# Projections and scores of an attention's first part, placed between the steps of the MLP in front of it

## The chip, the core and the metric

The kernel runs on one core of a Trainium2 chip. The metric is the device time of one execution in microseconds. Engines: TensorE (PE, its weight loads PEld), VectorE (DVE), ScalarE (ACT), GpSimd (POOL), SyncE (SP, which here issues all DMAs).

## The reference, cut to what matters

Four small transformer blocks run one after the other on x of 4 batches x 256 rows x 256 columns. Only the order and the shapes bear on this case.

```python
x = L0(ctx, x)      # 16-head attention over 512 keys, rms norm, MLP (m0)
x = L1(x, ctx)      # two attentions with 16 heads of 128 (b11, b12), layer norm, MLP (m1)
# L2, all heads 16 wide:
h = layernorm(x, ln1)                       # norm l21
q, k, v = split(h @ w_qkv + b_qkv)          # self attention: parts 0 to 3 of stage a2
s = q @ k.T / sqrt(16); s = s * mask - 10000 * (1 - mask)
x = x + softmax(s) @ v @ w_ao + b_ao
h = layernorm(x, ln2)                       # norm l22
x = x + attention(h @ w_q, enc @ w_kv, cross_mask) @ w_co   # parts 4 to 7 of a2
x = x + gelu(layernorm(x, ln3) @ w1) @ w2   # norm l23, MLP m2
# L3: no norm ahead of it
q, k, v = x @ Wq, enc @ Wk, enc @ Wv        # 32 query heads of 8, 8 key heads: stage a3
x = layernorm(softmax(q @ k.T / sqrt(8) + mask) @ v @ Wo + x)
```

## The kernel before, in words

Everything stays in SBUF; x lies as rows in `x_rows`, and what feeds a projection lies transposed in `hT`. The stages follow each other as a0, m0, b11, b12, m1, a2, m2, a3. Each engine has its own program, and semaphores tie them; the order on each engine is written out by hand.

**A small-head attention** (`attention(c)`, one function on each engine; `SMALL[1]` is a2 with 8 parts, `SMALL[2]` is a3 with 4) works on parts, one batch each, and a part on units: 16 in a2, 32 in a3, 128 in all in both. TensorE's `slot(s)` issues at slot s: scores of four units if s is a multiple of 4 (`scores`, L532, into banks 0 to 3, once the earlier four are out of them), the transposes of a unit some slots older (L545, banks 4 and 5), the product with v of four units (`times_v`, L567, bank 6), and, at fixed places of a part, the projections q, k and v of the next part (`project`, L502, L511, L517) and the output projection (L585). In a2 VectorE multiplies the scores with the mask (`times_mask`, L1103, four units at once) and takes the maxima (`maxima`, L1121); in a3 the mask is added, by L1121 alone. ScalarE does the exponentials (`exps`, L888) and copies the transposed units (`turned`, L896); VectorE shares the copies in a3 (L1129). VectorE also evacuates q (`queries`, L1067) and v (`values`, L1085), ScalarE k (`keys`, L875). All projections but those of part 0 go through bank 7, and so do the transposed rows of a norm: who comes next waits until the one before is evacuated (`before(m)`, `free`). `bank_of(m)` gives the banks of part 0: q 7, k 6, v 4.

**The host.** The MLP in front leaves the rows of its last batch normed (`norm_rows`, L1041; for a3 there is no norm) but not transposed. The attention does it (`c.host`, `normed(slot)`): slot 0 issues the four transposes (L464, bank 7), and ScalarE copies them to `hT` (`take_rows`, L856) after its first exponentials. Part 1's q projection, at slot 3 in a2 and slot 2 in a3, needs bank 7 and so this copy.

**An MLP** (`mlp`) runs over 4 batches, and over 10 steps f of each: steps 0 to 7 issue the first layer's tile f (L655, bank f mod 4; ScalarE's gelu, L921), steps 2 to 9 the second layer's tile f - 2 (L666, banks 4 and 5). At step 5 of a batch the normed rows of the batch before are transposed through bank 7. m2 also issues, in its batch 0, the last slots of a2. VectorE adds the result to `x_rows` (L1213) and takes its statistics (L1007, L1012, L1022). Only when m1 or m2 is through, and its last gelu and addition too, does TensorE begin the attention with q, k, v of part 0.

**POOL** does, in a fixed order, the power of each norm (L1354), the addition of a bias row to `x_rows` (L1349) and the conversion of a mask into its additive form (`additive`, L1343, L1345). SP loads the masks once the maxima that used the buffer are done.

## Time and profile before

| | us |
|---|---|
| median of 3 runs | 1602.65 |
| lowest, highest | 1600.52, 1605.79 |
| the profiled execution | 1607.07 |
| its span, first to last instruction | 1605.0 |

| engine | busy us | share of the span |
|---|---|---|
| TensorE matmul | 1493.2 | 93% |
| VectorE | 949.4 | 59% |
| ScalarE | 908.1 | 57% |
| POOL | 85.3 | 5% |

The shares are means over stages with different limits; the rows below go stage by stage. m1 ends at about 1073 us of the span, a2 runs to about 1326, m2 to about 1391, a3 to the end. A busy TensorE is one whose pipeline holds a matmul; the 0.17 us by which a group of matmuls seems to overlap the next is its latency. The short `READ_ACCUMULATOR` instructions between the maxima and exponentials are part of them.

### The profile page before, as it was taken

What the parts mean: (1) busy time and instruction counts of PE and PEld (TensorE: products, weight loads), DVE (VectorE), ACT (ScalarE), POOL (GpSimd) and SP (SyncE); (2) the same over time, 40 slices, a digit from 0 to 9 for tenths busy, and PEclk for the clock granted to TensorE, in tenths of its full rate; (3) what the DMA queues carried; (4) which work ended last, traced back from release to release, by engine and by line L of the source; (5) the groups of instructions that cost most, each with busy time, mean ns of one, the idle gap of its engine ahead of it and who ended that gap; (6) DMA issues with size and microseconds to landing.
All of it is one profiled execution on the core that took longest, in us unless ns stands there. A gap on an engine that the chain in (4) does not pass through costs nothing.

```text
span 1605.0 us, 28634 instructions
## 1 busy us (share of the span) xinstructions
PE 1493.2 (93%) x9824; PEld 1146.4 (71%) x9824; DVE 949.4 (59%) x3398; ACT 908.1 (57%) x2803; POOL 85.3 (5%) x89
## 2 busy tenths in 40 slices
PE   7999999999999999999999999997888879888886
PEld 5666687788787777778787878775656557755554
DVE  4777624545454455544455455238999991278885
ACT  5788824444444344444344444327888884388896
POOL 2000010000000001000000000110010010100000
PEclk9999999999999999999999999998999999999998
DMA  7000103010100101001010000010001000000000
GB/s 283 2 2 2 62 1 118 1 47 15 47 15 1 61 1 60 1 1 60 1 61 1 1 0 1 1 53 1 2 1 41 8 8 7 0 2 8 21 2 14
DMA packets 10878, 40.64 MB, mean 25 GB/s; under 512 B 2416, under 2 KB 2672, under 8 KB 8688
## 3 DMA queue, kind: packets, MB, share of 16 engines
q1 hardware_dynamic: 10736, 38.82, 6.8%
q8 instruction: 80, 1.31, 0.3%
q14 instruction: 62, 0.51, 0.1%
HBM read 37.77 MB, written 1.05 MB: 24 GB/s over the span
## 4 chain that ended last, share of the span: by engine, by line
PE 68%; DVE 11%; ACT 6%; issue 5%; DVEq 0%; POOLq 0%; POOL 0%; ACTq 0%
PE bank L726 7%; PE bank L707 7%; PE bank L740 7%; PE bank L699 7%; PE bank L686 7%; PE bank L689 7%; PE bank L666 5%; PE bank L655 5%; PE bank L715 4%; PE bank L545 3%; DVE probs L1121 3%; ACT probs L888 3%; DVE probs L1103 3%; PE bank L532 3%; DVE q_res L1067 2%
## 5 line engine op out<-in xcount | busy, mean ns | idle before, releaser
L888 ACT ACTIVATE probs<-probs,negmax 128x256 f32<-128x256 f32 (+1 forms) x640 | 346.9, 549 | 78.3 <-DVE negmax L1121 77.9
L959 ACT ACTIVATE pT<-bank 128x512 f32<-128x512 f32 x128 | 76.5, 597 | 387.8 <-PE bank L715 387.8
L545 PEld LDWEIGHTS bank<-ident,probs 128*128 128x128 f32 x1536 | 175.5, 145 | 110.6 <-issue 55.1
L545 PE MATMUL bank<-ident,probs 128*128 128x128 f32 x1536 | 232.4, 287 | 23.1 <-DVE pT L1129 12.5
L1236 DVE TENSOR_REDUCE stats<-bank 128x1 f32<-128x257 f32 x256 | 108.4, 425 | 212.4 <-PE bank L707 211.4
L1121 DVE CUSTOM_DVE_ANT_0 probs<-bank,mask_a 128x256 f32<-128x256 f32 (+1 forms) x384 | 176.2, 508 | 37.6 <-PE bank L532 33.4
L896 ACT ACTIVATE pT<-bank 128x512 f32<-128x512 f32 x304 | 178.1, 587 | 33.1 <-PE bank L545 32.9
L726 PE MATMUL bank<-pT,probs 128*128 128x256 f32 x512 | 132.6, 381 | 2.7 <-ACT pT L959 2.7
L707 PE MATMUL bank<-kT,pT 128*128 128x257 f32 x512 | 132.7, 382 | 0.6 <-ACT pT L942 0.6
L532 PE MATMUL bank<-kT,q_res 32*128 32x256 f32 (+1 forms) x1280 | 114.8, 465 | 17.0 <-DVE negmax L1121 13.8
L888 ACT ACTIVATION_READ_ACCUMULATOR probs<-probs,negmax 128x1 f32 x640 | 126.1, 197 | 0.0
L950 ACT ACTIVATE probs<-bank,stats 128x257 f32<-128x257 f32 x256 | 118.7, 474 | 3.5 <-DVE stats L1239 3.5
L726 PEld LDWEIGHTS bank<-pT,probs 128*128 128x128 f32 x512 | 95.8, 190 | 19.5 <-ACT pT L959 3.7
L707 PEld LDWEIGHTS bank<-kT,pT 128*128 128x128 f32 x512 | 96.3, 190 | 17.9 <-issue 3.2
L921 ACT ACTIVATE pT<-bank,cols 128x256 f32<-128x256 f32 x96 | 45.1, 474 | 107.7 <-PE bank L655 107.6
L1121 DVE CUSTOM_DVE_ANT_0 probs<-probs,mask_a 128x256 f32<-128x256 f32 x256 | 102.4, 451 | 0.0
L655 PE MATMUL bank<-hT,w_m 128*128 128x256 f32 x384 | 96.4, 382 | 1.3 <-DVE negmax L1121 1.3
L666 PE MATMUL bank<-w_m,pT 128*128 128x256 f32 x384 | 95.2, 379 | 0.3 <-ACT pT L921 0.3
L532 PEld LDWEIGHTS bank<-kT,q_res 32*128 32x128 f32 x1280 | 58.8, 192 | 45.4 <-issue 22.0
L1354 POOL TENSOR_TENSOR rstd<-ms,half 128x2 f32<-128x2 f32 x32 | 23.3, 729 | 1221.7 <-DVE ms L1022 1107.7
L1103 DVE TENSOR_TENSOR probs<-bank,mask_m 128x512 f32<-128x512 f32 x128 | 79.3, 681 | 9.8 <-PE bank L532 9.8
L1250 DVE TENSOR_SCALAR probs<-probs,stats 128x257 f32<-128x257 f32 x256 | 79.0, 351 | 4.5
(107 smaller groups left out, 2445.1 us busy)
## 6 DMA issues: line engine op xcount, KB each, us to landing
w_m<-in_w SPq DMA_DIRECT2D x6, 1024.0 KB, 7.1
g_qkv<-in_g SPq DMA_DIRECT2D x4, 1536.0 KB, 7.3
q_res<-in_g SPq DMA_DIRECT2D x4, 1536.0 KB, 6.3
w_qkv<-in_w SPq DMA_DIRECT2D x3, 768.0 KB, 4.3
g_bv<-in_gbv SPq DMA_DIRECT2D x8, 256.0 KB, 6.7
g_o<-in_go SPq DMA_DIRECT2D x4, 512.0 KB, 3.4
q_res<-in_go SPq DMA_DIRECT2D x4, 512.0 KB, 3.4
rows<-in_rows SPq DMA_DIRECT2D x1, 1664.0 KB, 14.0
```

Source lines behind the costliest of these rows:

```text
L532: last = mm(out, q_res[at, p % 2, i * c.res + r, q * P:(q + 1) * P], kT[at, p % 2, i % c.ktiles, 0:c.kv * P], start=True, stop=True)
L545: last = nc.tensor.transpose(out[:, n * P:(n + 1) * P], probs[:, u % PROBS, q * T + t * P:q * T + (t + 1) * P], ident[:, :])
L655: last = mm(bank[f % 4][:, 0:T], w_m1[:, k, f * P:(f + 1) * P], hT[:, b, k, :], start=(k == 0), stop=(k == KT - 1))
L666: last = mm(bank[4 + q][:, 0:D], h1T[:, f - 2, q * P:(q + 1) * P], w_m2[:, f - 2, :], start=(f == 2), stop=(f == FT + 1))
L686: mm(out[:, 0:T], g_qkv[g % 2][:, 1, k, h * P:(h + 1) * P], ctxT[:, b, k, :], start=(k == 0), stop=(k == KT - 1))
L707: mm(bank[q][:, 0:K1], qT1[:, n % 2, q * P:(q + 1) * P], kT1[:, n % 2, :], start=True, stop=True).then_inc(sem("b_scores"), 1)
L726: last = mm(bank[PV_BANK][:, 0:T], v1[:, u % 2, t, h * P:(h + 1) * P], pT1[:, n % 2, t, :], start=(t == 0), stop=(t == QT - 1))
L888: last = nc.scalar.activation(s, s, ACT.Exp, bias=negmax[:, u % PROBS, k:k + 1], scale=-1.0, accum_out=sums[:, tile % 2, q, j * c.res + r: ...
L896: nc.scalar.activation(pT[:, u % TURNED, :], bank[4 + u % 2][:, :], ACT.Copy).then_inc(sem("a_tout"), 1)
L950: last = nc.scalar.activation(probs1[:, n % 2, q, :], bank[q][:, 0:K1], ACT.Exp, bias=stats1[:, n % 2, 1, q:q + 1], scale=scale, accum_out ...
L1103: v.tensor_tensor(probs[:, u % PROBS, :], bank[u % QUAD][:, :], mask_m[:, mask_side(p), :], ALU.mult).then_inc(sem("a_masked"), 1)
L1121: last = v.tensor_tensor_reduce(out[:, at], src[:, at], mask_a[:, mask_side(p), at], -c.scale, HIGHEST, ALU.add, ALU.min, negmax[:, u % PR ...
```

## The change

For a2 and a3, TensorE issues the projections of part 0 between the steps of the last batch (b = 3) of the MLP in front: q at steps 1 and 2, k at 3 and 4, v at 7 and 8, and slot 0 (scores of units 0 to 3) at step 9, ahead of the last second-layer matmuls. Part 0 now has q in bank 6, k in 7, v in 6. ScalarE empties k behind the gelu of step 4, and TensorE waits for that before it transposes rows in bank 7 at step 5. VectorE empties q and v ahead of the last batch's addition. The host's rows are transposed at slot 10 instead of slot 0; in a2 VectorE norms them at its slot 3, behind the products of units 4 to 7, and makes the products of units 0 to 3 one by one between the maxima. POOL's order is written by slots: the host's bias comes with slot 12, the masks of a3 for batches 0 and 1 are converted at slots 117 and 133 of a2 instead of late in m2. The first exponentials of a tile wait for `a_inv` instead of `a_recip`. The waits of TensorE for the MLP's last gelu and addition move to step 9 and to the first transposes; the waits for the weights and for `s_rows` move ahead of the MLP.

```diff
     def normed(self, slot):
-        got = [-1] if slot == 0 and self.host else []
+        got = [-1] if slot == 10 and self.host else []
...
     def bank_of(self, m):
-        return [7, 6, 4, 5, 7][m] if m < len(self.loads()) else 7
+        return ([6, 7, 6] if self.host else [7, 6, 4, 5, 7])[m] if m < len(self.loads()) else 7
...
# TensorE, slot(s), at s == c.turn_lag
+                        else:
+                            pe.wait_ge(sem("m_out"), end("m1" if c.name == "2" else "m2", "m_out", B))
...
# TensorE, mlp, at each step f
                                 rows_turned(pe, own, b - 2)
+                            if b == B - 1 and project:
+                                k = S["a2" if n == 1 else "a3"]
+                                pe.wait_ge(sem("a_kout"), k.at("a_kout", 0, 1))
                             turn_rows(own, b - 1, bank[7])
+                        if b == B - 1 and project:
+                            if f == 1:
+                                if n == 1:
+                                    pe.wait_ge(sem("b_oout"), end("b12", "b_oout"))
+                                else:
+                                    pe.wait_ge(sem("a_oout"), end("a2", "a_oout"))
+                                project("q", 0, 0)
+                            elif f == 2:
+                                project("q", 0, 1)
+                            elif f == 3:
+                                rows_turned(pe, own, b - 2)
+                                project("k0", 0, 0)
+                            elif f == 4:
+                                project("k0", 0, 1)
+                            elif f == 7:
+                                project("v0", 0, 0)
+                            elif f == 8:
+                                project("v0", 0, 1)
+                            elif f == 9:
+                                pe.wait_ge(sem("m_gelu"), st.at("m_gelu", b, FT))
+                                following(0)
...
# ScalarE, exps
                     if tile >= 2 and u % (c.units // 2) == 0:
-                        act.wait_ge(sem("a_recip"), st.at("a_recip", 0, tile - 1))
+                        act.wait_ge(sem("a_inv"), st.at("a_inv", 0, tile - 1))
...
# ScalarE, mlp, behind the gelu of step f
+                        if b == B - 1 and f == NORM_AT - 1 and keys:
+                            keys("k0", 0)
...
# VectorE, attention
-                queries(0)
-                if c.host:
-                    norm_rows(c.host, B - 1, x_rows)
...
                 if c.kinds == "mult":
-                    for u in range(QUAD):
-                        times_mask(u)
+                    times_mask(0)
                 for slot in range(c.last_slot() + 1):
                     if slot < c.count:
                         maxima(slot)
-                        if c.kinds == "mult" and slot % QUAD == 3 and slot + 1 < c.count:
+                        if c.kinds == "mult" and slot < 3:
+                            times_mask(slot + 1)
+                        elif c.kinds == "mult" and slot % QUAD == 3 and slot + 1 < c.count:
                             for u in range(slot + 1, slot + 1 + QUAD):
                                 times_mask(u)
+                    if slot == 3 and c.host:
+                        norm_rows(c.host, B - 1, x_rows)
...
# VectorE, mlp
                         norm_rows(own, b - 1, x_rows)
+                    if b == B - 1 and queries:
+                        queries(0)
+                        values("v0", 0)
                     added(dve, f"m{n}", b)
...
# POOL
+            def after2(slot):
+                c = SMALL[1]
+                if slot == 12:
+                    pool.wait_ge(sem("l_z"), S["l21"].at("l_z", 0, B))
+                    bias("o2s", B - 1)
+                    additive(c, "2c", 0)
...
+                for b, x in enumerate([7 * c.units, 8 * c.units]):
+                    if slot == x + 5:
+                        additive(SMALL[2], "3", b)
...
+            def after3(slot):
+                c = SMALL[2]
+                if slot == 12:
+                    pool.wait_ge(sem("l_t"), S["l3t"].at("l_t", 0, B))
+                    bias("o3", B - 1)
...
```

## Rows read from the trace of the kernel before

**Rows 1.** Windows of three stretches: length, busy of PE, PEld, DVE, ACT, POOL, clock.

```profile
1040.00:1073.50 33.50, 33.50 (x160) 29.15 (x158) 5.38 (x18) 11.27 (x24) 3.93 (x4) 1.00 0.01 1
...
1090.50:1122.00 31.50, 25.98 (x239) 18.47 (x236) 30.50 (x111) 26.81 (x89) 0.00 (x0) 0.99 0.01 1
...
1409.50:1440.00 30.50, 26.23 (x266) 18.17 (x270) 24.86 (x119) 29.06 (x104) 0.00 (x0) 0.94 0.01 2
```

**Rows 2.** Timeline in MLP m1: start, us, engine, line, operation, [idle before, releaser].

```profile
1062.54 1.03 PE L655 MATMUL bank<-hT,w_m 128*128 128x256 f32 x4
...
1063.40 1.03 PE L666 MATMUL bank<-w_m,pT 128*128 128x256 f32 x4
1063.60 0.47 ACT L921 ACTIVATE pT<-bank,cols 128x256 f32<-128x256 f32 x1 [1.25 <-PE bank L655]
```

**Rows 3.** Timeline of the seam from m1 to a2.

```profile
1070.74 2.75 PE L666 MATMUL bank<-w_m,pT 128*128 128x256 f32 x12
...
1075.69 0.17 DVE L1022 TENSOR_SCALAR ms<-mv 128x2 f32<-128x2 f32 x1
...
1078.35 0.84 ACT L875 ACTIVATE kT<-bank,cols 128x256 f32<-128x256 f32 x2 [6.93 <-PE bank L511]
1078.44 0.73 DVE L1041 TENSOR_SCALAR y_rows<-x_rows,mv,rstd 128x256 f32<-128x256 f32 x2
...
1079.97 1.15 PE L532 MATMUL bank<-kT,q_res 32*128 32x256 f32 x16
...
1081.05 0.65 PE L464 MATMUL bank<-ident,y_rows 128*128 128x128 f32 x4
1081.21 2.48 DVE L1103 TENSOR_TENSOR probs<-bank,mask_m 128x512 f32<-128x512 f32 x4 [0.25 <-PE bank L532]
...
1085.41 1.00 ACT L856 ACTIVATE hT<-bank,cols 128x256 f32<-128x256 f32 x2
...
1086.46 2.07 PE L502 MATMUL bank<-hT,w_qkv 128*128 128x256 f32 x4 [4.76 <-ACT hT L856]
...
1088.47 2.09 PE L532 MATMUL bank<-kT,q_res 32*128 32x256 f32 x16
...
1090.57 2.48 DVE L1103 TENSOR_TENSOR probs<-bank,mask_m 128x512 f32<-128x512 f32 x4 [4.12 <-PE bank L532]
...
1094.78 0.42 DVE L1121 CUSTOM_DVE_ANT_0 probs<-probs,mask_a 128x256 f32<-128x256 f32 x1
```

**Rows 4.** Timeline of the seam from m2 to a3.

```profile
1388.81 2.75 PE L666 MATMUL bank<-w_m,pT 128*128 128x256 f32 x12
...
1395.34 1.00 PE L517 MATMUL bank<-w_qkv,ctxT 128*128 128x64 f32 x8
...
1398.61 1.15 PE L532 MATMUL bank<-kT,q_res 32*128 32x256 f32 x16 [2.27 <-DVE q_res L1067]
...
1399.85 0.42 DVE L1121 CUSTOM_DVE_ANT_0 probs<-bank,mask_a 128x256 f32<-128x256 f32 x1 [0.74 <-PE bank L532]
...
1402.64 0.63 ACT L856 ACTIVATE hT<-bank 128x256 f32<-128x256 f32 x2
...
1405.80 2.09 PE L532 MATMUL bank<-kT,q_res 32*128 32x256 f32 x16
1405.91 3.71 DVE L1067 TENSOR_SCALAR q_res<-bank,cols,marks 128x256 f32<-128x256 f32 x8 [3.21 <-PE bank L502]
...
1409.54 0.41 DVE L1121 CUSTOM_DVE_ANT_0 probs<-bank,mask_a 128x256 f32<-128x256 f32 x1
```

**Rows 5.** Window after the longest TensorE wait of the seam; last but two: granted clock.

```profile
1086.40:1088.40 2.00, 1.94 (x4) 1.17 (x4) 0.05 (x2) 1.98 (x9) 0.00 (x0) 0.50 0.00 0
```

**Rows 6.** Timeline of ScalarE in a2: the end of its packed stretch.

```profile
1121.62 0.51 ACT L888 ACTIVATE probs<-probs,negmax 128x256 f32<-128x256 f32 x1 [1.46 <-DVE negmax L1121]
```

**Rows 7.** Timelines of POOL and of VectorE, one moment in a2.

```profile
1208.01 0.85 POOL L1343 TENSOR_SCALAR mask_a<-mask_m 128x512 f32<-128x512 f32 x1 [6.04 <-DMA mask_m<-in_mask_2c]
...
1208.30 0.83 DVE L1121 CUSTOM_DVE_ANT_0 probs<-probs,mask_a 128x256 f32<-128x256 f32 x1
```

More of the change, by code:

```diff
@@ L620, in slot, with mlp @@
                             project(what, p, n)
-                for what in c.loads():
-                    project(what, 0, 0)
-                    project(what, 0, 1)
-                return slot
-            def mlp(n, before, own, after=None, c=None):
+                if c.name == "0":
+                    for what in c.loads():
+                        project(what, 0, 0)
+                        project(what, 0, 1)
+                return slot, project
+            def mlp(n, before, own, after=None, c=None, following=None, project=None):
                 st = S[f"m{n}"]
@@ L822, in _ @@
             c = SMALL[0]
-            slot = attention(c)
+            slot, _ = attention(c)
             for s in range(c.count + 2):
@@ L877, in keys, with attention @@
                     last.then_inc(sem("a_kout"), 1)
+                return keys
+            def attention(c):
+                st, keys = S["a" + c.name], keys_of(c)
                 def exps(u):
@@ L896, in turned @@
                     nc.scalar.activation(pT[:, u % TURNED, :], bank[4 + u % 2][:, :], ACT.Copy).then_inc(sem("a_tout"), 1)
-                for what in c.loads():
-                    if what[0] == "k":
-                        keys(what, 0)
+                if c.name == "0":
+                    for what in c.loads():
+                        if what[0] == "k":
+                            keys(what, 0)
                 for slot in range(c.count + c.copy_lag):
@@ L913, in attention, with mlp @@
                             keys(what, p)
-            def mlp(n, gelu, before, own):
+            def mlp(n, gelu, before, own, keys=None):
                 st = S[f"m{n}"]
@@ L1086, in values, with attention @@
                     last.then_inc(sem("a_pout"), 1)
+                return queries, values
+            def attention(c):
+                st = S["a" + c.name]
+                queries, values = projections_of(c)
+                dst = y_rows if c.name == "0" else x_rows
                 def mask_side(p):
@@ L1200, in attention, with mlp @@
                                 values(what, p)
-            def mlp(n, before, own):
+            def mlp(n, before, own, queries=None, values=None):
                 st = S[f"m{n}"]
@@ L1384, in _ @@
                 power_and_bias("l1m", b, "m1")
+            def after2(slot):
+                c = SMALL[1]
+                if slot == 12:
+                    pool.wait_ge(sem("l_z"), S["l21"].at("l_z", 0, B))
+                    bias("o2s", B - 1)
+                    additive(c, "2c", 0)
+                for b, x in enumerate([4 * c.units, 5 * c.units, 6 * c.units]):
+                    if slot == x + 5:
+                        additive(c, "2c", b + 1)
+                for b, x in enumerate([7 * c.units, 8 * c.units]):
+                    if slot == x + 5:
+                        additive(SMALL[2], "3", b)
+                for p, x in enumerate(c.parts):
+                    if slot == c.after(c.y_slot(p) + 1):
+                        power(x.norm, x.b)
+                    if slot == c.after(c.y_slot(p) + 1) + 3:
+                        pool.wait_ge(sem("l_z"), S[x.norm].at("l_z", 0, x.b + 1))
+                        bias("o2c" if x.norm == "l22" else "m2", x.b)
@@ L1385, in _ @@
+            def after3(slot):
+                c = SMALL[2]
+                if slot == 12:
+                    pool.wait_ge(sem("l_t"), S["l3t"].at("l_t", 0, B))
+                    bias("o3", B - 1)
+                for b in (2, 3):
+                    if slot == (b - 1) * c.units + 5:
+                        additive(c, "3", b)
+                for p, x in enumerate(c.parts):
+                    if slot == c.after(c.y_slot(p) + 1):
+                        power(x.norm, x.b)
             additive(SMALL[1], "2", 0)
-            for b in range(B):
+            for b in range(B - 1):
@@ L1402, in _ @@
+            for slot in range(SMALL[1].last_slot() + 1):
+                after2(slot)
+            for b in range(B - 1):
                 pool.wait_ge(sem("l_t"), S["l3t"].at("l_t", 0, b + 1))
                 bias("o3", b)
-            additive(SMALL[2], "3", 2)
-            power("l3", 0)
-            additive(SMALL[2], "3", 3)
-            for b in range(1, B):
-                power("l3", b)
+            for slot in range(SMALL[2].last_slot() + 1):
+                after3(slot)
 def _layouts(i):
```

56 lines of the change are left out of this document (19 added, 37 removed).

## The prediction

> **What bounds the kernel now.** I first cut the span by stage and read each engine's busy time in one stretch of each [rows 1]. Inside an MLP TensorE is busy 33.50 of 33.50 us and VectorE 5.38: TensorE alone sets the time there, and whatever is put on it lengthens the stage. In the attention a2 that follows m1, VectorE is busy 30.50 of 31.50 us: it sets the time. In a3, after m2, ScalarE leads with 29.06 of 30.50, close to VectorE and TensorE. So work moved from an attention to the MLP in front changes places: free for VectorE and ScalarE, dear for TensorE.
>
> Then I read the timeline over the two seams. I count from E, the end of the MLP's last matmul, to the start of the maxima of unit 4. Scores come in fours; before unit 4 the pipeline fills, after it its usual rhythm has begun, and projections and maxima there are the same in both kernels.
> - m1 to a2: E is 1070.74 + 2.75 = 1073.49; the maxima of unit 4 start at 1094.78, 21.29 us later [rows 3].
> - m2 to a3: E is 1388.81 + 2.75 = 1391.56, unit 4 starts at 1409.54, 17.98 us later [rows 4].
>
> In both the chain runs: residual add, q, k, v projections, evacuation, scores 0 to 3, then a TensorE wait for the host's rows (the transposed last rows, which ScalarE copies to hT behind its first exponentials), then part 1's q and scores 4 to 7.
>
> **Part 1: what the MLP's last batch gains on TensorE.** A 128x256 product of two instructions takes 0.43 us: L655's four instructions start at 1062.54, the next group at 1063.40 [rows 2].
> - a2: q, k, v are 24 instructions of 0.2155 = 5.17. Scores 0 to 3 occupy TensorE from 1079.97 to 1081.05 = 1.08 [rows 3].
> - a3: q 8 x 0.2155 = 1.72; k is one tile, 0.86; v eight narrow ones, 1.00 in the row with the last one's tail, 0.86 without [rows 4]; scores 1.08.
> - The added wait in step 5, for a_kout: bank 7 must be emptied of keys before the rows are turned in it. Queued behind it on TensorE are the transposes and all of steps 5 to 9. ScalarE starts gelu 0.20 after the group that feeds it has been issued [rows 2], 0.37 later the keys, 0.84 for two tiles [rows 3], so 1.47 with the semaphore; TensorE has 0.86 of second-layer matmuls meanwhile. It waits 0.61 in m1, and about 0.24 in m2, where one tile costs half. The bounds are 0 and the whole 0.84.
> - VectorE's evacuations (1.82 for a2, 3.7 for a3, values under 1 us) lie in its idle time, and the v projection in step 7 needs the bank of q more than four steps after q's end. Cost nothing; the cover is VectorE's 28 idle us [rows 1].
> - The waits for gelu, b_oout, a_oout and s_rows name things long done: nothing.
>
> Sum: m1 ends 5.17 + 1.08 + 0.61 = 6.86 later, m2 1.72 + 0.86 + 0.86 + 1.08 + 0.24 = 4.76 later.
>
> **Part 2: from the new E to unit 4.**
> a3: the residual add is over and the first maximum starts at about 0.95; four maxima of 0.69 give 3.72; part 1's q has long been projected, since the bank is free at once, and its evacuation takes 3.63 (1405.91 to 1409.54) [rows 4]. Scores 4 start on TensorE at 3.8, ahead of that. Unit 4 starts at 7.35. With part 1: 12.11 against 17.98, a gain of 5.87.
>
> a2: the statistics end at 2.37 (1075.86). Product and maximum now alternate, each waiting for the other's result: 0.68 + 0.69 + 0.04 = 1.41, so the fourth product is done and TensorE released at 2.37 + 3 x 1.41 + 0.68 + 0.06 = 7.34. I take 2.10. Behind it VectorE has four products 2.40, the host's norm 0.67 (0.73 less the overlap; now here, by the new place at slot 3) and part 1's queries 1.81 (from 1090.57 + 2.40 to 1094.78): 14.32. With part 1: 21.18 against 21.29. The gain is 0.11; 0.97 at full clock. The seam is merely refilled: what leaves the gap goes onto a busy TensorE.
>
> The Trainium skill, "TensorE: Matmul & The Clock Gate", section "HAM oscillation — how this bites in real kernels", says that an array that waits between bursts starts each next burst at half rate. It speaks for the lower value here; by it the first scores of both seams would be slow, and a3's gain would be 0.9 smaller. The trace has it after the wait of 4.76 us and, at the scores of 1405.80 (2.09), in a3 after its rows' wait, and not at 1398.61 [rows 3, 4].
>
> **Part 3: slot 10.** The host's four transposes, ScalarE's two copies and the bank-7 wait move from a time when all wait to the running pipeline.
> - a2: the copies take 1.00 [rows 3]. ScalarE is packed there until it waits 1.46 us for VectorE at 1121.62 [rows 6]; that would absorb them, but the v projection of slot 13 waits for the copy, and VectorE for v and the scores behind it. Bounds 0 and 1.4; I take 0.8, near the copy's own time.
> - a3: copies 0.63 [rows 4] on the engine with 1.44 idle of 30.5 us [rows 1]. Bounds 0 and 1.1 (with the transposes' 0.45); I take 0.6.
>
> **Part 4: POOL's order.** A POOL operation beside a maximum with both inputs in SBUF stretches it: a mask conversion at 1208.01, and the maximum at 1208.30 took 0.83 for the usual 0.42 [rows 7]. Mask 3,0 is now converted at about slot 114 of a2, where VectorE is the bound, and not in m2: +0.4. Mask 3,1 comes after the last maxima, in idle time: nothing, nor does the power behind it wait, as its y comes ten slots later. The bias o2s of batch 3 falls beside the queries evacuation, out of PSUM; mask 2c,0 follows it and can touch unit 4: bounds 0 and 0.4, taken 0.2. The Trainium skill, "GPSIMD Engine Reference", section "8. Key points", speaks against this part: POOL and VectorE share SBUF interfaces and contend when the VectorE instruction has two SBUF inputs. By it a3's maxima, with one input in PSUM, would be spared by bias o3 at slot 10; counting them as hit would add 1.0.
>
> The exps' wait for a_inv in place of a_recip is met eight units earlier either way: nothing. SP's queue keeps its order.
>
> **Sum.** a2: -0.11 + 0.8 + 0.4 + 0.2 = +1.3. a3: -5.87 + 0.6 = -5.3. Together -4.0 us. The profiled run took 1607.07 (span 1605.0), 4.4 above the median of three, 1602.65; it would be 1603.1, and the median 1598.6.
>
> **The rivals.**
> - *A, the seams close better*: scores 4 of a2 at full clock (-0.86), copies in slot 10 hidden (-1.4), POOL clear of VectorE (-0.6), and in a3 no low clock in the k projection of part 1 (-0.6). For: both engines then idle less than before. Against: the gap in a2 is longer, not shorter. -7.5: 1595.2.
> - *B, a3's head start leaks away*: after unit 4 three engines are nearly full, and TensorE, freed late by slot 10 with its bank-7 chain, holds the scores back; half of 5.87 is lost. -1.1: 1601.6. For: 29.06 of 30.50 on ScalarE. Against: unit 4 finds all engines in the state they had before.
> - *C, slower: the clock.* The low clock after a2's longer gap, and after a3's two shorter ones, lasts through the refill up to slot 12. TensorE works 25.98 of 31.50 us in the 16 units after the refill [rows 1], so 13 of 15.7 us up to slot 12; at half rate 26, so +10 in each. It decides from 9 us more half-rate work on the path than today. 1598.6 + 10 to 20, say 1610. For: 0.50 in [rows 5]. Against: before, full clock returned within 4 us of work.
> - *D, the change does nothing*: evacuations in the MLP hold up TensorE in steps 5 and 7 as much as a3 gains (+4): 1602.7.
>
> **How the numbers follow.** Forecast 0.45, A 0.22, B 0.16, C 0.07, D 0.06; 0.04 for others. The forecast's own range from the bounds is -6.5 to -2. The range for 8 in 10 leaves out C and A's far end: 1594 to 1603.5. A measurement of this kernel tells 0.3%, 4.8 us, from no change; the bound is 1597.8, just below the forecast. Faster: A's 0.20 and 0.16 of the forecast = 0.36. Same: the rest of the forecast, B, D and others = 0.54. Slower: C and a little of D = 0.10.
>
> **What would show it.** Part 1: m1's last batch longer by 6.9 us, m2's by 4.8, with a wait of 0.6 and 0.2 before step 5's transposes. Part 2: from the new E to unit 4 about 14.3 and 7.4 us, scores 4 of a2 lasting 2.1. Part 3: an idle stretch of VectorE of 0.8 before the values of part 1 in a2. Part 4: one more maximum of 0.8 near the end of a2. It is wrong if unit 4 of a3 starts more than 14 us after the old E, or if a2, from unit 4 on, is longer by more than 2.5.

## The result, and the profile after

| us | before | after |
|---|---|---|
| median (12 runs each, side by side) | 1602.42 | 1598.73 |
| lowest, highest | 1600.52, 1605.79 | 1595.55, 1601.26 |
| profiled execution | 1607.07 | 1601.26 |
| its span | 1605.0 | 1599.1 |

The ratio is 0.9978, with a 95% interval of 0.997 to 0.9987: 0.2% faster, or 3.5 us (2.1 to 4.8). That is inside the 0.3% which the forecast called "the same", and 0.1 us from the predicted 1598.6. With an interval 2.7 us wide, that the two agree to 0.1 us is luck.

The lines of the changed kernel: L464, L502, L511, L517, L532, L545 and L567 are TensorE's as before. L685 and L696 are the MLP's two layers (L655, L666 before), L1260 the residual addition (L1213), L1103 `queries` (L1067), L1121 `values` (L1085), L1146 `times_mask` (L1103), L1164 the maxima (L1121), L903 `keys` (L875), L883 `take_rows` (L856), L1077 `norm_rows` (L1041). In some experiments the lines of the other engines stand one to four higher.

The timeline over m1's last batch and the seam into a2, lines on the path only (start, us, engine, line, operation; in brackets the idle time before it and what ended it):

```profile
1066.80 1.03 PE L696 MATMUL bank<-w_m,pT 128*128 128x256 f32 x4
...
1067.38 0.83 ACT L903 ACTIVATE kT<-bank,cols 128x256 f32<-128x256 f32 x2
...
1068.31 0.63 PE L464 MATMUL bank<-ident,y_rows 128*128 128x128 f32 x4 [0.48 <-issue]
...
1076.64 1.15 PE L532 MATMUL bank<-kT,q_res 32*128 32x256 f32 x16
...
1077.71 1.13 PE L696 MATMUL bank<-w_m,pT 128*128 128x256 f32 x4
...
1078.96 0.76 DVE L1260 TENSOR_TENSOR x_rows<-bank,x_rows 128x256 f32<-128x256 f32 x2 [2.19 <-PE bank L696]
...
1085.39 0.69 DVE L1146 TENSOR_TENSOR probs<-bank,mask_m 128x512 f32<-128x512 f32 x1
...
1086.12 2.09 PE L532 MATMUL bank<-kT,q_res 32*128 32x256 f32 x16 [6.42 <-DVE probs L1146]
...
1088.14 2.08 PE L502 MATMUL bank<-hT,w_qkv 128*128 128x256 f32 x4
1088.23 2.48 DVE L1146 TENSOR_TENSOR probs<-bank,mask_m 128x512 f32<-128x512 f32 x4 [1.35 <-PE bank L532]
...
1090.63 0.73 DVE L1077 TENSOR_SCALAR y_rows<-x_rows,mv,rstd 128x256 f32<-128x256 f32 x2
...
1091.28 1.89 DVE L1103 TENSOR_SCALAR q_res<-bank,cols,marks 128x256 f32<-128x256 f32 x4
...
1093.09 0.59 DVE L1164 CUSTOM_DVE_ANT_0 probs<-probs,mask_a 128x256 f32<-128x256 f32 x1
```

Three things are to be seen. The transposes of step 5 (L464) start 1.51 after the group ahead of them, which has 0.86 of work: TensorE waits 0.65 for ScalarE's keys (0.83, from 1067.38). Scores 0 to 3 run at 1076.64, ahead of the MLP's last four matmuls; these end at 1077.71 + 1.13 = 1078.84, which is the new E. And the wait of 4.76 us for the host's rows in [rows 3] is gone, but another of 6.42 stands in its place: TensorE waits for VectorE's fourth product, then runs scores 4 and the second half of part 1's q at the low clock (2.09 and 2.08). Unit 4 starts at 1093.09, 14.25 after E.

The same view of the seam from m2 to a3:

```profile
1384.74 1.03 PE L696 MATMUL bank<-w_m,pT 128*128 128x256 f32 x4
...
1385.32 0.47 ACT L903 ACTIVATE kT<-bank,cols 128x256 f32<-128x256 f32 x1
...
1385.88 0.63 PE L464 MATMUL bank<-ident,x_rows 128*128 128x128 f32 x4
...
1394.45 1.13 PE L696 MATMUL bank<-w_m,pT 128*128 128x256 f32 x4
...
1395.42 1.89 PE L502 MATMUL bank<-hT,w_qkv 128*128 128x256 f32 x8
1395.69 0.76 DVE L1260 TENSOR_TENSOR x_rows<-bank,x_rows 128x256 f32<-128x256 f32 x2 [2.38 <-PE bank L696]
1396.37 0.41 DVE L1164 CUSTOM_DVE_ANT_0 probs<-bank,mask_a 128x256 f32<-128x256 f32 x1
...
1399.12 3.71 DVE L1103 TENSOR_SCALAR q_res<-bank,cols,marks 128x256 f32<-128x256 f32 x8
...
1399.25 1.15 PE L532 MATMUL bank<-kT,q_res 32*128 32x256 f32 x16 [1.94 <-DVE negmax L1164]
...
1402.74 0.41 DVE L1164 CUSTOM_DVE_ANT_0 probs<-bank,mask_a 128x256 f32<-128x256 f32 x1
```

Here TensorE waits only 1.94, and scores 4 run at full clock. Unit 4 starts at 1402.74, 7.16 after E at 1395.58. VectorE goes without a break from maximum to q_res to maximum; in [rows 4] it had waited 3.21 for part 1's q.

To compare kernels I measured the starts of the same events in every trace, from the start of the addition (L1260) of the MLP's batch 2, the last addition that the change leaves alone. "Last batch" is the distance to batch 3's addition, "unit n" the one to its first maximum. "Low" is the time, idle time included, at the 1.2 GHz level of the granted clock from that addition to unit 16 of a2, in two parts.

```
us                before  after  x1     x2     x3     x4     x5     x7     x8     x9     x10    x11    x12
m1's last batch   14.25   21.38  14.25  21.38  21.37  21.37  21.38  20.10  18.38  14.25  14.25  14.25  14.25
a2 unit 4         35.43   35.50  35.43  35.50  37.95  35.50  34.56  34.24  32.38  35.43  31.87  31.87  31.87
a2 unit 8         41.49   43.25  41.50  41.57  44.02  42.99  42.24  40.30  40.12  41.50  40.32  40.31  40.85
a2 unit 12        47.21   48.96  47.21  47.28  49.73  48.70  47.95  46.02  45.83  47.21  46.04  46.03  46.56
a2 unit 16        53.94   56.81  53.95  56.69  56.47  58.11  57.36  55.42  55.24  53.94  53.87  53.86  54.38
low to unit 4      6.8     6.8    6.8    6.8   10.2    7.2    0      6.8    3.4    6.8    1.7    1.7    0.7
low, unit 4 to 16  0       3.4    0      3.4    0      6.5    6.8    3.4    6.8    0      5.1    5.1    6.2
m2's last batch   14.25   19.31  19.31  14.25  19.31  19.31  19.32  18.04  17.15  18.04  19.31  14.25  18.04
a3 unit 4         32.12   26.36  26.36  33.28  26.36  31.88  26.36  25.52  25.28  25.52  26.36  29.69  25.52
a3 unit 16        48.43   43.11  43.10  49.55  43.12  47.13  43.14  42.27  42.00  41.53  43.10  46.48  42.26
```

**The ledger of the two spans**, 1605.0 and 1599.1, is -5.9: -1.78 lies ahead of the changed code (batch 2's addition in m1 comes at 1059.36 and at 1057.58, same instructions; before had 3.4 us of low clock there, after none), +0.74 between that addition and the one in m2, and -4.91 from there to the end. The changed part gives -4.2, the medians -3.7.

One term of POOL's order was to show near the end of a2, and does:

```profile
1301.37 0.79 POOL L1392 TENSOR_SCALAR mask_a<-mask_m 128x512 f32<-128x512 f32 x1 [6.44 <-DMA mask_m<-in_mask]
...
1301.60 0.82 DVE L1164 CUSTOM_DVE_ANT_0 probs<-probs,mask_a 128x256 f32<-128x256 f32 x1
```

Mask 3,0 is converted at 1301.37, and the maximum beside it takes 0.82 for 0.42. Mask 3,1 (1329.50) falls into idle time, as forecast.

### The profile page after: what moved, and what is told of

It reads as the page before. It is cut to its first block, busy times and chain, and to the rows that moved or that the text cites. A ratio compares the mean times of both kernels' runs of the same rounds, so it can differ in the third digit from the quotient of the medians.

```text
span 1599.1 us, 28632 instructions
## 1 busy us (share of the span) xinstructions
PE 1490.4 (93%) x9824; PEld 1145.4 (72%) x9824; DVE 950.8 (59%) x3398; ACT 908.5 (57%) x2803; POOL 85.5 (5%) x89
## 4 chain that ended last, share of the span: by engine, by line
PE 68%; DVE 11%; ACT 6%; issue 5%; DVEq 0%; POOLq 0%; POOL 0%; ACTq 0%
PE bank L756 7%; PE bank L737 7%; PE bank L770 7%; PE bank L729 7%; PE bank L716 7%; PE bank L719 7%; PE bank L696 5%; PE bank L685 5%; DVE probs L1164 4%; PE bank L745 4%; PE bank L545 4%; ACT probs L921 3%; DVE probs L1146 3%; PE bank L532 2%; PE bank L567 1%
## 5 line engine op out<-in xcount | busy, mean ns | idle before, releaser
L545 PEld LDWEIGHTS bank<-ident,probs 128*128 128x128 f32 x1536 | 176.1, 146 | 111.3 <-issue 57.5
L545 PE MATMUL bank<-ident,probs 128*128 128x128 f32 x1536 | 232.8, 288 | 23.4 <-DVE pT L1172 12.8
L1164 DVE CUSTOM_DVE_ANT_0 probs<-bank,mask_a 128x256 f32<-128x256 f32 (+1 forms) x384 | 176.3, 509 | 36.2 <-PE bank L532 32.0
L532 PE MATMUL bank<-kT,q_res 32*128 32x256 f32 (+1 forms) x1280 | 113.6, 461 | 23.0 <-DVE negmax L1164 15.5
L1164 DVE CUSTOM_DVE_ANT_0 probs<-probs,mask_a 128x256 f32<-128x256 f32 x256 | 103.4, 455 | 0.1
L685 PE MATMUL bank<-hT,w_m 128*128 128x256 f32 x384 | 96.2, 380 | 2.4 <-DVE negmax L1164 2.4
L696 PE MATMUL bank<-w_m,pT 128*128 128x256 f32 x384 | 96.1, 380 | 0.3 <-ACT pT L955 0.3
L532 PEld LDWEIGHTS bank<-kT,q_res 32*128 32x128 f32 x1280 | 58.4, 190 | 51.1 <-DVE negmax L1164 23.4
L1146 DVE TENSOR_TENSOR probs<-bank,mask_m 128x512 f32<-128x512 f32 x128 | 79.7, 683 | 7.1 <-PE bank L532 7.0
```

The costliest lines, as they stand in the source:

```text
L532: last = mm(out, q_res[at, p % 2, i * c.res + r, q * P:(q + 1) * P], kT[at, p % 2, i % c.ktiles, 0:c.kv * P], start=True, stop=True)
L545: last = nc.tensor.transpose(out[:, n * P:(n + 1) * P], probs[:, u % PROBS, q * T + t * P:q * T + (t + 1) * P], ident[:, :])
L685: last = mm(bank[f % 4][:, 0:T], w_m1[:, k, f * P:(f + 1) * P], hT[:, b, k, :], start=(k == 0), stop=(k == KT - 1))
L696: last = mm(bank[4 + q][:, 0:D], h1T[:, f - 2, q * P:(q + 1) * P], w_m2[:, f - 2, :], start=(f == 2), stop=(f == FT + 1))
L1146: v.tensor_tensor(probs[:, u % PROBS, :], bank[u % QUAD][:, :], mask_m[:, mask_side(p), :], ALU.mult).then_inc(sem("a_masked"), 1)
L1164: last = v.tensor_tensor_reduce(out[:, at], src[:, at], mask_a[:, mask_side(p), at], -c.scale, HIGHEST, ALU.add, ALU.min, negmax[:, u % PR ...
```

## The experiments

All are edits of the changed kernel ("after"); the diffs are cut to their core. x1 to x4 ran on one chip, x5 to x9 on another occasion, and x10 to x12 on a third, each beside its own runs of before; before's medians were 1601.32, 1601.56 and 1601.69. Ratios are to these.

### x1 and x2: each seam alone

```diff
# x1: a3's seam as in after, a2's as before (x2: the other way round)
-        got = [-1] if slot == 10 and self.host else []
+        got = [-1] if self.host and slot == {'2': 0, '3': 10}[self.name] else []
...
-                if c.name == "0":
+                if c.name in ("0", "2"):          # x2: ("0", "3")
                     for what in c.loads():
                         project(what, 0, 0)
...
-            mlp(1, "l1m", "l21", following=slot, project=project)
+            mlp(1, "l1m", "l21")
```

> The change at the seam m2 to a3 alone; a2 starts as in the kernel before. Theory (all of the gain is a3's restart, a2's seam is refilled and costs a little in the running pipeline): from the addition of batch 2 in m1 to the maxima of unit 4 of a2 35.4 us, as before; from the addition of batch 2 in m2 to unit 4 of a3 26.4 us instead of 32.1; the whole 5 us faster than before, 1597.4, so no slower than the full change. Rival (both seams gain about half of the 3.7 us each): 1600.6, slower than the full change by 1.9.

> The change at the seam m1 to a2 alone; a3 starts as in the kernel before. Theory: unit 4 of a2 at 35.5 us, within 0.3 of before, then 1 to 2.8 us lost up to unit 16 (the k projection at the low clock, the copy of the host's rows in slot 10), part of it won back; the whole 0 to +1.5 us, 1602.4 to 1604. Rival (both seams gain): 1600.6.

x1: 1594.76 (6 runs), 0.9965 [0.9953, 0.9977], that is -5.6 us (-3.7 to -7.5). x2: 1603.62 (11 runs), 1.002 [1.001, 1.003], +3.2 us (1.6 to 4.8). The seam of a3 carries the whole gain, and the seam of a2 costs: more than the 0 to +1.5 expected of x2 and the +1.3 of the forecast, which lies just below the interval. It takes back a good part of what a3 gives. At unit 16 of a2, x2 is 2.75 behind before. Its own part of that stretch that before does not have:

```profile
1106.01 1.93 PE L567 MATMUL bank<-pT,v_two 128*32 128x256 f32 x16
...
1109.27 0.43 DVE L1191 COPY recipT<-bank 128x256 f32<-128x256 f32 x1 [2.50 <-PE bank L575]
```

The product with v (L567) takes 1.93 at the low clock, and VectorE waits 2.50 for the transposed sums behind it. In after the same matmuls took 1.07 and the wait was 0.94, but there the low clock had fallen on the k projection, some eight units earlier:

```profile
1093.22 1.77 PE L511 MATMUL bank<-hT,w_qkv 128*128 128x256 f32 x4 [2.10 <-DVE q_res L1103]
...
1095.64 1.70 PE L511 MATMUL bank<-hT,w_qkv 128*128 128x256 f32 x4
...
1098.43 2.48 DVE L1146 TENSOR_TENSOR probs<-bank,mask_m 128x512 f32<-128x512 f32 x4 [2.32 <-PE bank L532]
```

The first half of k at 1093.22 takes 1.77, the second at 1095.64 takes 1.70 (in x1 1.13 and 1.03), and VectorE waits 2.32 for the scores queued behind. So both have a second stretch of low clock after unit 4, at different work; the windows of 21 us behind unit 4 show it, where x1, as before, has none. (Columns: the window, its length, busy time of PE, PEld, DVE, ACT, POOL, then granted clock, DMA share, GB/s.) First x1, then after, then x2:

```profile
1093.00:1111.50 18.50, 16.91 (x165) 11.80 (x166) 17.61 (x70) 17.50 (x61) 0.00 (x0) 1.00 0.01 1
```

```profile
1093.00:1114.40 21.40, 19.15 (x169) 13.50 (x170) 18.07 (x71) 18.69 (x62) 0.41 (x1) 0.92 0.01 2
```

```profile
1093.50:1114.70 21.20, 19.01 (x169) 12.93 (x170) 17.98 (x70) 18.77 (x63) 0.34 (x1) 0.92 0.01 2
```

A clock of 0.92 over 21 us is 3.4 us at half speed. The code of a2 is the same in after and x2, so it is the place of this stretch alone that makes units 4 to 8 take 7.75 and 6.07 us, and units 12 to 16 7.85 and 9.41.

### x3 and x4: the host's rows turned first, as before, with the early projections kept

```diff
# x3 for a2 ('2': 1), x4 for a3 ('2': 10, '3': 1)
-        got = [-1] if slot == 10 and self.host else []
+        got = [-1] if self.host and slot == {'2': 1, '3': 10}[self.name] else []
...
# x3 alone, VectorE
                 if c.kinds == "mult":
+                    norm_rows(c.host, B - 1, x_rows)
                     times_mask(0)
```

> The full change, but in a2 the host's rows are normed ahead of the products and turned at slot 1 instead of slot 10. Theory (slot 10 puts 1.0 us of ScalarE copies where VectorE waits behind them): unit 4 of a2 within 1 us of the full change (35.5: the norm is no longer behind the products, but its wait for the power, 0.8, is in the chain), and the wait of VectorE for TensorE ahead of part 1's outputs and values (0.94 in the full change) gone: the whole 0.5 to 2.5 us faster than the full change, 2.5 if the clock also holds since TensorE's gap is cut in two. Rival (ScalarE's slack of 1.46 us at the end of its packed stretch absorbs the copies anyway): no faster than the full change, and unit 20 at the same distance.

> The full change, but in a3 the host's rows are turned at slot 1. Part 1's q then waits for the copy behind the third exponentials. Theory (a3's gain comes from q of part 1 no longer waiting for the host's rows): unit 4 of a3 at about 30 us after the addition of batch 2 in m2 instead of 26.4; 0.6 won back later; the whole 3 us slower than the full change, 1601.7. Rival (the gain comes from the projections' place in the MLP, and slot 10 is only a detail): within 1 us of the full change.

x3: 1601.42 (11 runs), 0.9995 [0.9983, 1.0007]. x4: 1602.63 (11 runs), 1.0005 [0.9996, 1.0015]. x3 was expected to be 0.5 to 2.5 us faster than after and is 2.7 slower by the ratios; x4 is 4.3 slower, for the expected 3. Without slot 10 in a3 the gain of that seam is gone: unit 4 comes at 31.88 and not at 26.36. The timeline of x4 there:

```profile
1394.26 0.63 PE L464 MATMUL bank<-ident,x_rows 128*128 128x128 f32 x4 [1.01 <-DVE x_rows L1260]
...
1397.79 0.63 ACT L883 ACTIVATE hT<-bank 128x256 f32<-128x256 f32 x2
...
1398.47 3.78 PE L502 MATMUL bank<-hT,w_qkv 128*128 128x256 f32 x8 [3.59 <-ACT hT L883]
...
1402.29 3.71 DVE L1103 TENSOR_SCALAR q_res<-bank,cols,marks 128x256 f32<-128x256 f32 x8 [5.43 <-PE bank L502]
```

The chain of [rows 4] is back: transposes, then 3.59 of waiting for ScalarE's copy, then part 1's q, now at the low clock (3.78 for the 1.89 in after). In x3, unit 4 of a2 comes 2.45 later than in after, and units 12 to 16 take 6.74 for 7.85: slot 10 costs 1.11 in a2, the rows' place ahead of unit 4 cost 2.45. The expectation of x3 (unit 4 within 1 us) left out what POOL then does, since its bias row and mask follow the norm and now run beside the first maxima:

```profile
1085.82 1.27 POOL L1397 TENSOR_TENSOR x_rows<-x_rows,rows 128x512 f32<-128x512 f32 x1 [0.85 <-DVE y_rows L1077]
...
1086.37 1.00 DVE L1164 CUSTOM_DVE_ANT_0 probs<-probs,mask_a 128x256 f32<-128x256 f32 x1
```

This maximum takes 1.00 and the next 0.82, 0.98 more than twice 0.42; the norm and its wait for POOL's power put 1.5 more ahead of the fourth product, and part 1's q, at the low clock, holds scores 4 another 0.6; the norm's 0.7 behind the products is saved. In x4 the chain came out 2 us dearer in a3 than expected, by the low clock in part 1's q.

### x5: work without use in TensorE's long wait

```diff
                 def slot(s):
+                    if s == 4 and c.name == "2":
+                        pe.wait_ge(sem("a_pout"), st.at("a_pout", 0, c.evacuated("v0", 0)[1]))
+                        for _ in range(11):
+                            mm(bank[6][:, 0:T], ident[:, :], hT[:, 0, 0, :], start=True, stop=True)
```

> The full change, with 11 products more of 0.43 us (identity times rows nobody reads, into bank 6) on TensorE in a2's gap ahead of scores 4, so that it idles 1.7 us there instead of 6.4. Theory (what a2 loses behind unit 4 comes mostly of TensorE's granted clock): scores 4 take 1.15 instead of 2.09 and the k projection of part 1 its 1.1 instead of 1.8; unit 4 at 34.6 us after batch 2's addition in m1 instead of 35.5, unit 8 at 40.7 instead of 43.25, unit 16 at 54 to 55 instead of 56.8; the whole 1.5 to 2.5 us faster than the full change in the same state. Rival (the loss is slot 10's copies, the clock costs nothing as VectorE bounds): unit 16 no more than 0.9 earlier.

1596.34 (7 runs), 0.9965 [0.9952, 0.9977]: by the ratios 2.1 us ahead of after, near the expected 1.5 to 2.5, but with an interval that overlaps after's. TensorE's own lines of x5:

```profile
1081.44 4.91 PE L594 MATMUL bank<-hT,ident 128*128 128x256 f32 x22
1088.02 1.15 PE L532 MATMUL bank<-kT,q_res 32*128 32x256 f32 x16 [1.67 <-DVE probs L1150]
...
1094.17 2.07 PE L511 MATMUL bank<-hT,w_qkv 128*128 128x256 f32 x4 [3.08 <-DVE q_res L1107]
...
1106.85 1.25 PE L517 MATMUL bank<-w_qkv,hT 128*128 128x256 f32 x4 [1.17 <-ACT hT L887]
1108.03 1.93 PE L567 MATMUL bank<-pT,v_two 128*32 128x256 f32 x16
```

The 11 products, which nobody reads, fill 4.91 of the wait, and what follows ran at full clock, scores 4 in 1.15 instead of 2.09. Unit 4 came 0.94 earlier, as the theory of the clock wants. But unit 16 came at 57.36, later than after's 56.81, where the theory had it earlier: the k projection waited 3.08, took 2.07 for its first half, and L567 took 1.93 behind a wait of 1.17. Low clock up to unit 16 was 10.2 us in after and 6.8 in x5, but all of it now lay after unit 4. In this trace, then, the filler moved the slow stretch to a place where more waits for it. That it costs more there isn't shown: x4, whose a2 has the code of after, stands at 58.11 at unit 16, so that one code differs by 1.4 between traces, and the profiled execution of x5 (1601.32) was the slowest of its seven.

### x7, x8 and x9: less on TensorE ahead of E

```diff
# x7: scores 0 to 3 behind the MLP
-                                following(0)
+                                if n not in (1, 2):
+                                    following(0)
...
# x8: x7, and the v projection behind the MLP too
                 def slot(s):
+                    if s == 1 and c.name in ('2', '3'):
+                        project("v0", 0, 0)
+                        project("v0", 0, 1)
...
# x9: x1, with a3's scores behind the MLP, and POOL's masks of a3 back in m2
-                for b, x in enumerate([7 * c.units, 8 * c.units]):
-                    if slot == x + 5:
-                        additive(SMALL[2], "3", b)
```

> The full change, but slot 0 (the first scores) behind the MLP's last matmuls instead of ahead of them, at both seams. Theory (TensorE is the MLP's only bound, and these scores have cover behind it: the statistics in a2, the addition in a3): the last batch of m1 and m2 1.1 us shorter; unit 4 of a2 at 34.4 instead of 35.5, unit 4 of a3 at 25.8 instead of 26.4, since the addition hides only 0.8 of 1.24; the whole 1.7 us faster than the full change. Rival (moving the scores into the MLP is what starts the attention early): unit 4 of a3 1 us later.

> As the run with the scores behind the MLP, and the v projection of part 0 behind them too, evacuated by VectorE behind the maxima of unit 3. Theory: a2 gains its 1.72 us in full, since VectorE idles there for scores 4 (unit 4 at 32.7 instead of 35.5), and TensorE's idle stretch is shorter; a3 gains 0.1, 0.86 off TensorE against 0.73 on VectorE (unit 4 at 25.7); the whole 3.5 us faster than the full change. Rival (the gap behind m1 is full: VectorE takes the evacuation on its path): unit 4 of a2 at 33.6 or later.

> a2 as in the kernel before; at the seam to a3 the change with slot 0 behind the MLP; masks 3,0 and 3,1 converted in m2 again. Theory: the a3-only run less 0.6 (scores) and less 0.4 (POOL beside a maximum of a2): 6.6 us faster than the kernel before, 1594.7. Rival (a conversion on POOL costs VectorE nothing that lasts, and slot 0's place neither): as the a3-only run, 5.6 faster.

x7: 1596.51 (7 runs), 0.9967 [0.9955, 0.9979]. x8: 1596.06 (5 runs), 0.9962 [0.9948, 0.9976]. x9: 1595.55 (9 runs), 0.9965 [0.9953, 0.9978]. With the scores behind the MLP its last batch is 1.28 shorter in m1 and 1.27 in m2; unit 4 gains nearly all of that in a2 (1.26) and 0.84 in a3. The v projection behind it takes another 1.72 out of m1's last batch, of which 0.18 is left at unit 8: the k projection then runs at the low clock, 6.8 us of it behind unit 4. The traces show the gains at the seams; by the ratios x7 is 1.8 and x8 2.6 us ahead of after (expected 1.7 and 3.5), with intervals that overlap after's. x9, expected 1 us ahead of x1, can't be told from it.

### x10, x11 and x12: move the rows, leave the projections

```diff
# x10: a2's q, k, v behind m1 as before; its host's rows at slot 10, normed at slot 3 (a3 as in after)
-                if c.name == "0":
+                if c.name in ("0", "2"):
                     for what in c.loads():
                         project(what, 0, 0)
...
-            mlp(1, "l1m", "l21", following=slot, project=project)
+            mlp(1, "l1m", "l21")
...
-                    times_mask(0)
+                    for u in range(QUAD):
+                        times_mask(u)
# x11: the same in a3 too. x12: x10 with a3 as in x9
```

> a3's seam as in the full change; at a2's seam nothing is moved into m1, and only the host's rows are normed at VectorE's slot 3 and turned at slot 10. Theory (what held a2's refill up was the TensorE wait for the host's rows, and the projections moved into m1 only lengthen it): m1's last batch 14.25 us as before; scores 4 start when the fourth product is done, ahead of VectorE's need; unit 4 at 31.9 us after batch 2's addition in m1 instead of 35.4 before and 35.5 in the full change; 1.1 lost in slot 10; the whole 2.4 faster than the a3-only run, some 8 us (0.5%) faster than before. Rival (the gap behind m1 is that of VectorE's own chain, however the rows are placed): unit 4 at 34.5 or later, and the whole as the a3-only run.

> Nothing is moved into the MLPs; only the host's rows are turned at slot 10, at both seams. Theory: unit 4 of a2 at 31.9 us; unit 4 of a3 at 28.8 us after batch 2's addition in m2, between 32.1 before and 26.4 in the full change, since the projections in m2 bring the other 2.4; less 1.1 and 0.6 in slot 10; the whole 5 us faster than before, as fast as the full change or faster. Rival (the projections' place in the MLP carries the gain): unit 4 of a3 no earlier than 31, the whole within 1 us of before.

> As the run with a2's rows alone, and a3 with slot 0 behind m2's last matmuls, and masks 3,0 and 3,1 converted in m2. Theory: unit 4 of a3 at 25.5 us instead of 26.4, a maximum of a2 0.4 shorter: 1.2 us faster than that run, 9 us (0.6%) faster than before. Rival (after the refill TensorE's clock and the three nearly full engines take such small gains back): within 0.5 us of that run.

x10: 1594.86 (5 runs), 0.9958 [0.9942, 0.9973], the lowest ratio of all. x11: 1599.26 (11 runs), 0.9985 [0.9974, 0.9996]. x12: 1596.21 (5 runs), 0.9963 [0.995, 0.9975]. Against before that is 6.7 us for x10, where 8 was expected, and 5.9 for x12, where 9 was; x12 can't be told from x9 or x10. The seam of x10:

```profile
1081.32 1.15 PE L532 MATMUL bank<-kT,q_res 32*128 32x256 f32 x16
...
1082.39 1.13 PE L502 MATMUL bank<-hT,w_qkv 128*128 128x256 f32 x4
1082.56 2.48 DVE L1148 TENSOR_TENSOR probs<-bank,mask_m 128x512 f32<-128x512 f32 x4 [0.17 <-PE bank L532]
...
1085.10 1.15 PE L532 MATMUL bank<-kT,q_res 32*128 32x256 f32 x16 [1.57 <-DVE probs L1148]
...
1092.57 0.59 DVE L1166 CUSTOM_DVE_ANT_0 probs<-probs,mask_a 128x256 f32<-128x256 f32 x1
...
1092.71 2.07 PE L511 MATMUL bank<-hT,w_qkv 128*128 128x256 f32 x4 [4.16 <-DVE q_res L1105]
```

Part 1's q (L502 at 1082.39) follows scores 0 to 3 at once, where [rows 3] had 4.76 of waiting between; the four products run in one go and free TensorE after 1.57; scores 4 take 1.15. Unit 4 comes at 31.87, 3.56 earlier than in before: most of the 4.76 of [rows 3], which the early projections had paid away. Yet at unit 16 x10 stands at 53.87 and before at 53.94: the k projection (L511 at 1092.71, 2.07 for its first half, after a wait of 4.16) and what follows ran at the low clock for 5.1 us, and slot 10 takes its share. In x10, x11 and x12, then, a2 had lost its head start by unit 16; the forms with early projections stand there 1.3 to 4.2 us behind before. x10's advantage over x1, 0.1 us there, is no more than noise; x10 is the fastest by the ratio, but not shown to be faster than x1.

x11 against x10 prices a3's early projections: 0.0027 of the time, or 4.3 us (1.3 to 7.3, an estimate from the two intervals), and unit 4 of a3 at 29.69 for 26.36. The move of the rows alone gave a3 2.43 at unit 4, less than expected, and the kernel 2.4 us for the expected 5. Its scores 0 to 3 show something else:

```profile
1394.73 2.09 PE L532 MATMUL bank<-kT,q_res 32*128 32x256 f32 x16 [2.20 <-DVE q_res L1105]
```

The wait before them was 2.20 and they took 2.09, at the low clock. In [rows 4] the same instruction after 2.27 took 1.15. x2, with before's code there, had 2.19 and 2.09 too. So before's profile was better at this place than the others, by 0.94 in these scores and 1.16 at unit 4 (32.12 against x2's 33.28). Read against x2, a3's gain is 6.9 at unit 4 and not 5.8, and that of the rows alone is 3.59, no less than the expected 3.3.

## Why the prediction was right

The time was right, and so was the seam that gives it; the errors in a2 were small beside a3's gain.

- **What bounds.** Right. Each projection put into the MLP lengthened its last batch one for one, and x10 against after shows that in a2 nothing came of it.
- **Part 1.** Forecast 6.86 and 4.76, measured 7.13 (21.38 - 14.25) and 5.06 (19.31 - 14.25). The wait for the keys was 0.65 and 0.28, forecast 0.61 and 0.24. What is missing, 0.2 to 0.3, is the term for the scores: they take TensorE 1.07 (1076.64 to 1077.71), but without them the last batch is 1.28 shorter (x7). The rest are two steps of 0.10: the scores start 0.96 after the group ahead (1075.68), where other groups follow at 0.86, and the four matmuls behind them take 1.13 for 1.03.
- **Part 2.** E to unit 4: forecast 14.32 and 7.35, measured 14.25 and 7.16, in the order forecast: the product after each maximum, scores 4 at 2.09 after 6.42 of idle time (forecast 6.4), norm 0.73, queries 1.89. The gain of a3 at unit 4 is 5.76, forecast 5.87; a2's is -0.07, forecast 0.11.
- **The clock.** This is the term that the forecast had too small. I priced the low clock in scores 4 and let it end there, since unit 4 "finds all engines in the state they had before". It did not: a second stretch, 3.4 us, fell into the units behind. Unit 4 to 8 took 7.75 for 6.06, so 1.69. That was part of rival C's mechanism at a tenth of its price: C put the whole refill at half rate for 10 us or more. Up to unit 16 the three kernels that left this seam alone (before, x1, x9) have 6.8 us of low clock, all ahead of unit 4. In after, x2, x7 and x8 it is 10.2, in x3 too, but all ahead of unit 4, and in x4 13.7. x5, x10, x11 and x12 have 6.8 as well, but 5.1 or more of it behind unit 4, where more waits for TensorE. Which work is hit, the k projection (after) or the product with v (x2), changes from trace to trace of the same code.
- The Trainium skill, "TensorE: Matmul & The Clock Gate", section "HAM oscillation — how this bites in real kernels", has each burst after a wait start at half rate, for waits beyond a certain length; the prediction left that condition out. The traces agree for the long waits: in the 13 traces, from batch 2's addition in m1 to the end of a3, all eleven of 4 us and more (6.42, 5.15, 4.76, 4.16, 4.06) were followed by a granted clock of 0.50. Below that both levels occur. Of 83 waits of 3.0 to 3.6 us 57 were followed by full clock, among them one of 3.46 in x2 and most of a2's regular ones of 3.1; 21, among them x5's 3.08, were followed by half rate, and in five the clock changed within the first half microsecond. Waits near 2.2 us went both ways too. a3's scores 4 ran at full clock after 1.94 in all five traces that have this wait. Two of the regular waits, in after, both 3.11 us ahead of the same four transposes:

```profile
1203.13 1.11 PE L464 MATMUL bank<-ident,y_rows 128*128 128x128 f32 x4 [3.11 <-DVE v_two L1121]
...
1266.36 0.66 PE L464 MATMUL bank<-ident,y_rows 128*128 128x128 f32 x4 [3.11 <-DVE v_two L1121]
```

- **Part 3.** a2: forecast 0.8; units 12 to 16 took 7.85 for 6.73, so 1.12, and x3 gives it back. The idle stretch of VectorE ahead of part 1's values (L1121) is there, 0.94 for the forecast 0.8; the copy of hT at 1104.90 holds the v projection (L517), and this holds what is queued behind it:

```profile
1104.90 1.02 ACT L883 ACTIVATE hT<-bank,cols 128x256 f32<-128x256 f32 x2
...
1105.97 1.13 PE L517 MATMUL bank<-w_qkv,hT 128*128 128x256 f32 x4 [1.17 <-ACT hT L883]
...
1108.75 1.03 PE L517 MATMUL bank<-w_qkv,hT 128*128 128x256 f32 x4
1108.95 0.42 DVE L1189 COPY recipT<-bank 128x256 f32<-128x256 f32 x1 [0.94 <-PE bank L575]
...
1109.82 0.89 DVE L1121 TENSOR_TENSOR v_two<-bank,rows 128x128 f32<-128x128 f32 x4
```

  a3: forecast 0.6, and the gain shrinks from 5.76 at unit 4 to 5.32 at unit 16: 0.44.
- **Part 4.** Forecast 0.4 and 0.2. The maximum at 1301.60 took 0.82 (0.40 more), the one at 1093.09, beside mask 2c,0, 0.59 (0.17 more). Nothing of the 0.17 seems to last: x2, with 0.58 there, takes 6.07 from unit 4 to 8, before 6.06. In a3 a maximum with one input in PSUM kept its 0.42 (1410.63) beside POOL's bias row (1.28 from 1410.44), so that part was rightly put at nothing.
- **The sum.** a2 +1.3 forecast; by x2's timing +3.2 (1.6 to 4.8), so this term was too small. Up to unit 16 the forecast was 0.9 (the 0.4 of mask 3,0 comes later), the trace has 2.87: the clock's 1.69, 0.32 of slot 10. a3 -5.3 forecast; -5.32 at unit 16, by x1's timing -5.6, which contains POOL's +0.4. Sum -4.0 forecast, -3.5 measured (-4.8 to -2.1). Of the two signs of being wrong, unit 4 of a3 came 12.2 after the old E, well under 14. The other, a2 longer by more than 2.5 from unit 4 on, is passed at unit 16 (21.31 for 18.51, so 2.80) and no longer at unit 64 (0.86).
- **The rivals.** A, -7.5, lies outside the interval; it needed full clock in a2's scores 4, which took 2.09. B fell: the head start of a3 did not leak, 5.25 were left at unit 32 although ScalarE was then full (the window of [rows 1] in after, below: 30.48 of 30.50 us, for 29.06 before). D is ruled out by x1. C is the one of which a part came true.

```profile
1409.50:1440.00 30.50, 27.32 (x304) 18.55 (x303) 24.75 (x118) 30.48 (x110) 1.28 (x1) 1.00 0.04 8
```

What stays open: how much of the clock's cost lasts. From unit 16 to unit 32 of a2, in equal code, before spent 6.7 us at the low clock and after 3.1, and after's 2.87 behind at unit 16 shrank to 1.20 at unit 32 (85.71 and 86.91), about what 3.6 us at half rate are worth. Counted from batch 2's addition to unit 32, the low clock is 10.2 or 13.5 us in the three kernels with before's a2 seam, 10.2 to 13.7 in the three with after's (after, x2, x4), and 6.8 to 17.1 in the rest: so the second stretch is extra up to unit 16, and not shown to be extra beyond it. From that addition to the one in m2, before, x1 and x9 took 318.06, 314.51 and 316.80, and after, x2 and x4 318.80, 316.63 and 317.27: 1.1 more in the mean, nearer to the forecast than to x2's timing, but with 3.5 us between two kernels that have the same seam. The same holds ahead of the changed code: -1.78 in the ledger goes with 3.4 us at the low clock in before's profile and none in after's. Such stretches are as large as the effect of a2's seam, so a single profile can't settle that seam; only the ratio of x2 times it by itself, to about 1.6 us. The regular waits of 3.1 us, after which the clock is low in one trace and full in another, are one place where such stretches begin. What POOL's order does to the total was not timed by itself.

## What to carry to other kernels

Before moving work from a stage into the one in front, ask which engine bounds each: filling a gap with work of the engine that bounds the stage in front only moves that work, and the gain is what the gap holds beyond it. Split a wait into the chain that causes it: here the transposed rows of the host were most of it, and a later slot for them took it away by itself (x10; what that is worth in the whole is not shown, since x10's ratio can't be told from x1's), while the projections paid only at the seam where they stood in a chain with everything else (a3). Look further on, too: a head start at unit 4 was gone at unit 16. And time each half of a two-part change alone: behind the -3.5 stood -5.6 and +3.2.

## What the runs showed of the hardware

- A low clock that is paid once can come back. After the longest wait (6.42 us) the half-rate stretch was followed by a second, some 7 us after the first scores at half rate in after and some 19 in x2, in work that had run at full clock in before. Filling the wait (x5) took the first away; the one trace then has 6.8 us of it in two stretches behind unit 4.
- The length of a wait settles the granted clock behind it only from 4 us on here (half rate eleven times out of eleven). After 3.0 to 3.6 us 21 of 83 waits were followed by half rate and 57 by full clock, and around 2.2 us the same scores took 1.15 after 2.27 us (before) and 2.09 after 2.20 and 2.19 us (x11, x2).
- Scores put ahead of the last four matmuls of the MLP cost its end 1.28 us, though they hold TensorE for 1.07.
- A maximum with two inputs in SBUF took 1.00 and 0.82 for 0.42 beside POOL operations of 1.27 and 0.67 (x3); with one input in PSUM, beside one of 1.28, it kept its 0.42 (after).
